# Layer normalisation of a graph kernel: statistics kept in place of rows, rows made by ScalarE, conv1's weights prepared earlier

## The reference, cut to what matters

```python
h = maximum(layernorm(x), 0)                      # per node, eps 1e-5
# layer 0, a gated unit with two inputs
c = relu(bn1(conv1d(h.T, conv1_w)))               # 1 tap: 256x256
c = relu(bn2(conv1d(c, conv2_w, pad=8)) + h.T).T  # 17 taps
s = h @ w_se.T + b_se                             # 3 values a node
A = exp(-|s_n - s_m|^2) * adj
nmp = A @ relu(h @ w_msg.T + b_msg)
gi = concat(c, nmp) @ w_ih.T + b_ih ; gh = h @ w_hh.T + b_hh
r, z = sigmoid(gi_r + gh_r), sigmoid(gi_z + gh_z)
n = tanh(gi_n + r * gh_n)
x = x + (1 - z) * n + z * h
# layer 1
g = maximum(layernorm(x), 0)
x = x + relu(g @ w[:256] + (adj @ g) @ w[256:] + bias)
```

## Time and profile before

| | |
|---|---|
| median of the runs | 1807.4 us |
| the profiled execution | 1806.16 us, span 1804.4 us |
| granted TensorE clock, mean | 0.994 |
| PE busy | 1729.2 us (96%) |
| DVE busy | 1475.5 us (82%) |
| ACT busy | 884.0 us (49%) |
| POOL busy | 594.4 us (33%) |
| DMA queue of SP | 261.94 MB, 46.1% of 16 engines' span |

### The profile page before, as it was taken

The page is one execution under the profiler, slowest core; times in us unless marked ns, Lnnn a source line. Parts: engine busy times, 40 slices in busy tenths (PEclk is TensorE's granted clock), DMA queues, the critical chain, the costliest instruction groups (busy, mean ns, idle before and its releaser), DMA issues. The chain is left out here.

```text
span 1804.4 us, 36601 instructions
## 1 busy us (share of the span) xinstructions
PE 1729.2 (96%) x12221; PEld 1139.9 (63%) x12222; DVE 1475.5 (82%) x3194; ACT 884.0 (49%) x1617; POOL 594.4 (33%) x744
## 2 busy tenths in 40 slices
PE   3779999999998999999999999999999999999997
PEld 2467777764445666666666666666666666666664
DVE  6789888862346988888888888888888888888886
ACT  4665666665344444444444444444444444444442
POOL 5688777711012222222222222222222222222221
PEclk9899999999999999999999999999999999999999
DMA  6287888769743334334334334334334334334331
GB/s 241 77 302 262 290 304 281 256 230 340 258 141 121 96 100 116 94 100 116 94 100 116 94 101 115 94 101 115 94 102 115 93 104 115 92 105 115 92 107 33
DMA packets 242827, 262.70 MB, mean 146 GB/s; under 512 B 82392, under 2 KB 178639, under 8 KB 242255
## 3 DMA queue, kind: packets, MB, share of 16 engines
q1 hardware_dynamic: 242766, 261.94, 46.1%
HBM read 154.92 MB, written 90.18 MB: 136 GB/s over the span
## 5 line engine op out<-in xcount | busy, mean ns | idle before, releaser
L1568 PE MATMUL ps_rz<-big 128*128 128x512 f16 x2304 | 560.1, 379 | 0.8 <-DVE big L1561 0.8
L1568 PEld LDWEIGHTS ps_rz<-big 128*128 128x128 f16 x2304 | 221.9, 98 | 203.0 <-DVE big L1561 1.0
L1568 PE MATMUL ps_n<-big 128*128 128x256 f16 x2304 | 314.2, 273 | 0.2
L1568 PEld LDWEIGHTS ps_n<-big 128*128 128x128 f16 x2304 | 225.1, 98 | 95.2 <-DVE big L1705 1.2
L1568 PE MATMUL ps_l<-big 128*128 128x512 f16 (+1 forms) x1536 | 272.0, 327 | 8.8 <-DVE big L1807 4.5
L1279 PE MATMUL m_ps<-big 128*128 128x512 f16 (+1 forms) x1152 | 268.3, 375 | 3.2 <-DVE big L1046 2.4
L1736 POOL TENSOR_TENSOR big<-big 128x256 f32<-128x256 f32 x128 | 97.6, 763 | 450.7 <-ACT big L1729 450.7
L1568 PEld LDWEIGHTS ps_l<-big 128*128 128x128 f16 x1536 | 149.9, 98 | 97.2 <-DVE big L1807 5.5
L1568 PE MATMUL ps_b<-big 128*128 128x256 f16 x1536 | 189.9, 273 | 2.1 <-DVE big L1636 2.1
L1711 ACT ACTIVATE big<-big,w_scale 128x512 f32<-128x512 f32 x128 | 92.6, 724 | 177.0 <-DVE big L1702 177.0
L1279 PEld LDWEIGHTS m_ps<-big 128*128 128x128 f16 x1152 | 111.9, 98 | 105.3 <-issue 2.4
(11 more groups left out here) (240 smaller groups left out, 2802.9 us busy)
## 6 DMA issues: line engine op xcount, KB each, us to landing
spectra<-ysb SPq DMA_DIRECT2D x96, 256.0 KB, 3.7
big<-spectra SPq DMA_DIRECT2D x64, 384.0 KB, 3.4
xin<-in_x SPq DMA_DIRECT2D x64, 256.0 KB, 3.4
x_normed<-front SPq DMA_DIRECT2D x64, 256.0 KB, 2.3
h_turned<-front SPq DMA_DIRECT2D x64, 256.0 KB, 3.9
big<-h_turned SPq DMA_DIRECT2D x64, 256.0 KB, 2.7
big<-in_adj SPq DMA_DIRECT2D x64, 256.0 KB, 3.4
big<-in_x SPq DMA_DIRECT2D x64, 256.0 KB, 2.8
```

Source lines behind the costliest of these rows:

```text
L1568: last = pe.matmul(dest, stationary(dl), moving(wl), start=start and n == 0, stop=stop and n == 2, **kw)
```

## The change

Four things.
1. In the filters' stage DVE makes the scales and conv1's scaled weights before `square_rows(1)`, PE turns them before it spreads the row scales, ACT copies them before its first filter tiles, and the small values per channel are made inside the loop over tiles, after its third pair.
2. POOL's part per graph is the inverse root and, in place of the rows, a bias -mean x root, two instructions of 128x1. Mean (negated and scaled) and root of every graph stay in a tile `norm`.
3. ACT makes the rows xhat in the convolution, `normalise(q+1)` at the head of its slot q. They are not stored any more; the tile `norm` is, once (1 KB a partition), at unit 6 after the slots.
4. In the gates' stage the 16 bytes a partition of `norm` are loaded a graph in place of the rows, and ACT makes the rows again (`normed_rows`), after `weighted_high`.

```diff
@@ convolution_weights, scalar
-                act.wait_ge(scales_ready, 1)
-                tile_high(0)
-                tile_high(2)
                 act.wait_ge(w1_turned, 1)
                 act.activation(w1t[:, 0, :, 0:D], pz[3][:, 0, :].rearrange("p (h o) -> p h o", o=D),
                                ACT.Copy).then_inc(w1_high, 1)
                 act.activation(bias_m[:, :], pz[3][:, 1, 0:D], ACT.Copy).then_inc(w1_high, 1)
+                act.wait_ge(scales_ready, 1)
+                tile_high(0)
+                tile_high(2)
@@ convolution_weights, vector
-                square_rows(1)
                 dve.wait_ge(sums_seen, 1)
...
+                dve.tensor_scalar(cvec[:, 0:2], V(tmp, 0), sc[:, 4:5], None, ALU.mult)
+                then(dve.tensor_scalar(cvec[:, 2:4], V(tmp, 1), sc[:, 4:5], None, ALU.mult))
+                for h in range(H):
+                    dve.tensor_scalar(w1n[:, h, :], w1n[:, h, :], cvec[:, h:h + 1], None,
+                                      ALU.mult).then_inc(w1_scaled, 1)
...
+                square_rows(1)
                 dve.wait_ge(roots_made, 2)
...
+                    if b == 2:
+                        channel_values()
@@ convolution_weights, tensor
-                pe.wait_ge(scales_placed, 2)
-                for h in range(H):
-                    last = pe.matmul(pz[2][0:ROWS_T, 1, 0:NT], spread[:, h, 0:ROWS_T], placed[:, h, :],
-                                     start=h == 0, stop=h == H - 1)
-                last.then_inc(sums_seen, 1)
                 pe.wait_ge(w1_scaled, 4)
...
+                pe.wait_ge(scales_placed, 2)
+                for h in range(H):
+                    last = pe.matmul(pz[2][0:ROWS_T, 1, 0:NT], spread[:, h, 0:ROWS_T], placed[:, h, :],
+                                     start=h == 0, stop=h == H - 1)
+                last.then_inc(sums_seen, 1)
@@ convolution, sync
-                store_xhat(0)
                 load_x(3)
                 for q in range(SLOTS):
-                    if q + 1 < graphs:
-                        store_xhat(q + 1)
...
+                    if u == 6:
+                        sp.wait_ge(norm_signed, graphs)
+                        sp.dma_start(norm_d, norm[:, :, :, :].rearrange("p g h c -> p (g h c)")).then_inc(norm_stored, 16)
@@ convolution, gpsimd
-                def normalise(f):
+                def layer_bias(f):
                     pool.wait_ge(rstd_done, f + 1)
-                    if f >= 2:
-                        pool.wait_ge(turned, f - 1)
-                        pool.wait_ge(xhat_stored[f % 2], 16 * (f // 2))
                     for t in range(H):
-                        last = pool.tensor_scalar(xhat[:, f % 2, t, :], xin[:, f % 3, t, :], meanvar[:, f % 2, t, 0:1],
-                                                  rstd[:, f % 2, t:t + 1], ALU.subtract, ALU.mult)
-                    last.then_inc(xhat_done, 1)
+                        last = pool.tensor_scalar(norm[:, f, t, 0:1], norm[:, f, t, 0:1], norm[:, f, t, 1:2], -1.0,
+                                                  ALU.mult, ALU.mult)
+                    last.then_inc(norm_signed, 1)
@@ convolution, scalar
+                def normalise(f):
+                    act.wait_ge(norm_signed, f + 1)
+                    if f >= 2:
+                        act.wait_ge(turned, f - 1)
+                    for t in range(H):
+                        last = act.activation(xhat[:, f % 2, t, :], xin[:, f % 3, t, :], ACT.Identity,
+                                              scale=norm[:, f, t, 1:2], bias=norm[:, f, t, 0:1])
+                    last.then_inc(xhat_done, 1)
...
+                normalise(0)
                 for q in range(SLOTS):
+                    if q + 1 < graphs:
+                        normalise(q + 1)
                     if q < graphs:
                         split_h(q)
@@ convolution, vector, layer_stats(f)
-                    if f >= 2:
-                        dve.wait_ge(xhat_done, f - 1)
@@ gates, sync and scalar
+            before(sp, "rows_made", t, 1, 2)
             sp.dma_start(xin[:, p, :, :], x_d[t]).then_inc(x_loaded[p], 16)
-            before(sp, "diff_done", t, H, 2)
-            sp.dma_start(xhat[:, p, :, :].rearrange("p h d -> p (h d)"), xhat_d[t]).then_inc(xhat_loaded[p], 16)
+            sp.dma_start(norm[:, p, :, :].rearrange("p h c -> p (h c)"), norm_d[t]).then_inc(norm_loaded[p], 16)
+        def normed_rows(act, t, p):
+            arrived(act, x_loaded, t, p)
+            arrived(act, norm_loaded, t, p)
+            before(act, "diff_done", t, H, 2)
+            for i in range(H):
+                last = act.activation(rows_h[:, p, i, :], xin[:, p, i, :], ACT.Identity, scale=norm[:, p, i, 1:2],
+                                      bias=norm[:, p, i, 0:1])
+            last.then_inc(S["rows_made"], 1)
...
                         weighted_high(act, t, p)
+                        normed_rows(act, t, p)
```

More of the change, by code:

```diff
@@ L414, in _ @@
-                tile_low(2)
[L415 to L431, removed]
+                tile_low(2)
+                def channel_values():
+                    then(dve.tensor_scalar(V(tmp, 9), V(tmp, 9), 2.0 ** -(W_EXP + CONV_EXP + Y_EXP) * 2 / SPAN,
+                                           sc[:, 0:1], ALU.mult, ALU.mult))
+                    dve.tensor_tensor(cvec[:, 4:6], V(tmp, 2), V(tmp, 9), ALU.mult)
+                    dve.tensor_copy(cvec[:, 6:8], V(tmp, 3))
+                    then(dve.tensor_tensor(bound[:, 0, :], V(tmp, 2), V(tmp, 8), ALU.mult))
+                    then(dve.tensor_scalar(bound[:, 0, :], bound[:, 0, :], sc[:, 0:1], 2.0 * (TAPS * D) ** 0.5,
+                                           ALU.mult, ALU.mult))
+                    dve.tensor_tensor(bound[:, 1, :], V(tmp, 3), V(tmp, 3), ALU.mult)
+                    then(dve.tensor_tensor(bound[:, 0, :], bound[:, 0, :], bound[:, 0, :], ALU.mult))
+                    then(dve.tensor_tensor(bound[:, 0, :], bound[:, 0, :], bound[:, 1, :], ALU.add))
+                    dve.tensor_tensor(cvec[:, 9:10], bound[:, 0, 0:1], bound[:, 0, 1:2], ALU.add)
@@ L477, in _, with convolution @@
                         last.then_inc(w_done, 1)
-def convolution(nc, ident, big, w1t, bias_m, dt_sb, cvec, s_all, a, xin, x_loaded, y_d, h_d, xhat_d, pair_d, w, early):
+def convolution(nc, ident, big, w1t, bias_m, dt_sb, cvec, s_all, a, xin, x_loaded, y_d, h_d, norm_d, pair_d, w, early):
     x = a["x"]
@@ L541, in convolution @@
         h_stored = [sem(f"h_stored{i}") for i in range(2)]
-        xhat_stored = [sem(f"xhat_stored{i}") for i in range(2)]
+        norm_signed = sem("norm_signed")
+        norm_stored = sem("norm_stored")
         fwd_done = sem("fwd_done")
@@ L1018, in layer_stats @@
                     for t in range(H):
-                        last = dve.bn_aggr(meanvar[:, f % 2, t, :], stats[:, f % 2, t, :])
+                        last = dve.bn_aggr(norm[:, f, t, :], stats[:, f % 2, t, :])
                     last.then_inc(stats_done, 1)
@@ L1419, in sem @@
             return ctx.enter_context(nc.semaphore(name))
-        xin, xhat, adj_in, rows = early.xin, early.xhat, early.adj_in, early.rows
+        xin, norm, rows_h, adj_in, rows = early.xin, early.norm, early.rows_h, early.adj_in, early.rows
         inv, ht, pairs = early.inv, early.ht, early.pairs
@@ L1740, in x1_rows @@
             ready(dve, "n_tanh", t, i + 1, H)
-            arrived(dve, xhat_loaded, t, p)
-            dve.scalar_tensor_tensor(out=diff[:, i, :], in0=xhat[:, p, i, :], scalar=0.0, in1=new[:, i, :],
+            ready(dve, "rows_made", t)
+            dve.scalar_tensor_tensor(out=diff[:, i, :], in0=rows_h[:, p, i, :], scalar=0.0, in1=new[:, i, :],
                                      op0=ALU.max, op1=ALU.subtract).then_inc(S["diff_done"], 1)
```

63 lines of the change are left out of this document (31 added, 32 removed).

## The result

| | before | after |
|---|---|---|
| median of the runs | 1807.66 us (4 runs) | 1889.91 us (1888.7 to 1890.4, 4 runs) |
| ratio | 1 | 1.0454, 95% interval 1.0441 to 1.0467 |
| profiled execution | 1806.16 us, span 1804.4 | 1890.4 us, span 1888.2 |
| PE busy, granted clock | 1729.2 us, 0.994 | 1754.9 us, 0.986 |
| DMA of SP's queue | 261.94 MB | 228.64 MB |

A forecast was written before the change was run, and what follows sets the result against it. PE, busy 96%, bounded the old kernel; a new loop of waits would outlast its slots. 1806.2 + 81.6 (slots) + 0.9 (beginning) - 1.0 (filters) = 1887.7, about 1888 as median; 8-of-10 range 1850 to 1915.

The forecast's parts named there:

- The ring's path and length: Convolution slots: waits from DVE's aggregate through GpSimd's bias, ACT's normalise and split_h, back to DVE, 5.91 us every slot.
- The held add: GpSimd's add L832: held by DVE's two-SBUF-input instruction, 0.544 against 0.194; the bias pair stays short, taken as 0.55 us.
- The rival of the short loop: Convolution slots: add not held, bias pair and normalise shorter, so 5.05 us a slot, +28, time 1835; chance 0.12.
- The number of turns: Convolution: the new loop of waits comes round 62 times from split_h(1) to split_h(63).
- The extra of heavy slots: Heavy convolution slots: split_y ahead of add_bias adds about 0.6 in one of four, mean 0.17 us a slot.
- The sum of the slots: Convolution, split_h(1) to split_h(63): 374.1 us where the old kernel takes 292.5, so +81.6.
- The beginning: Up to split_h(1): the first turn comes earlier, but split_h(1) now waits for normalise(2); +0.9 us.
- The stores: Convolution and unit 6: storing no rows, and one small store at unit 6 instead, is worth 0.
- The gates' rows: Gates' stage: ACT's 0.91 us a graph fits in 1.48 idle, 0; rival without cover +58, time 1945, chance 0.03.
- The filters' stage: Filters' stage: PE starts 2.3 to 3.7 earlier, channel_values cost 1.6 to 3.0 in DVE's loop; net -1 us.
- the 1887.7 of the sum: Whole kernel: profiled 1806.2 + 81.6 + 0.9 - 1.0 us; about 1888 as median of runs.
- The rival of the clock: Light convolution slots: TensorE drops to 1.2 GHz, 7.1 us a slot, +20, time 1908 or more; chance 0.10.

The follow-up runs named there:

- e2_pool: The kernel after the change, but GpSimd makes the convolution's rows as before: 1808.29 us, 1.0002 of the kernel before.
- e8_rows_twice: The kernel after the change, with ACT making each graph's rows twice in the gates' stage: 1892.21 us, 1.0468 of the kernel before.
- e7_pool_values: As e1_behind, but GpSimd makes the values per channel after its last pair of tiles, not DVE inside its loop: 1801.96 us, 0.9965 of the kernel before.
- e1_behind: The kernel after the change, with split_h(q) ahead of normalise(q+1) on ACT: 1805.53 us, 0.9987 of the kernel before.
- e4_stats_first: The kernel after the change, with layer_stats(q+2) ahead of split_h(q) on DVE, ACT's order kept: 1823.79 us, 1.0083 of the kernel before.
- e6_early_alone: The kernel before with only the change's filters' stage: 1810.10 us, 1.0009, against 1808.68 for the kernel before beside it.

## Why the prediction was right, step by step
- **The ring's path and length.** 5.91 forecast, 5.94 measured. The bias took 0.53 (0.55 taken); normalise from SBUF 1.00 (0.91 taken, from the form that reads PSUM; it came out near the upper end of the 0.60 to 1.02 considered: 593 ns each and 560 from PSUM); the hand-offs were those of the earlier trace rows within 0.03. Two small misses of opposite sign.
- **The held add.** L833 has 0.54 as before, since it still starts beside DVE's L1047, and 0.20 in the three turns at the start where it does not. The bias pair takes 0.50, but not for the reason given: in light slots no DVE instruction runs beside it, since L1054, which was L1046, ends at 127.35 and the pair starts at 127.34. The reason is tested only in heavy slots, half of which have an instruction with one input in PSUM beside the whole pair, and there it holds:
```profile
303.80 0.68 DVE L1059 SCALAR_TENSOR_TENSOR ysb<-m_ps,ysb 128x512 f16<-128x512 f32 x1
303.88 0.50 POOL L841 TENSOR_SCALAR norm<-norm 128x1 f32<-128x1 f32 x2
```
  The rival of the short loop, which needed L832 at 0.19, falls.
- **The number of turns.** The sum has 62 turns; the ring has 61. Behind the normalise of graph 63 no other comes, so nothing stands ahead of split_h(63), and the last distance is 3.82 us and not 5.9:
```profile
450.66 1.09 ACT L918 ACTIVATE front<-xin,norm 128x256 f32<-128x256 f32 x2 [0.53 <-POOL norm L841]
451.66 0.57 ACT L927 ACTIVATE front<-turn_ps 128x512 f16<-128x512 f32 x1
...
455.48 0.59 ACT L927 ACTIVATE front<-turn_ps 128x512 f16<-128x512 f32 x1
```
- **The extra of heavy slots.** 0.17 on average forecast; 5.94, 5.94, 5.95 and then 6.54 measured, 0.60 in one slot of four, the one with split_y ahead of add_bias. The mean of the 44 turns is 6.12, so 0.18.
- **The sum of the slots.** 374.1 forecast, 455.48 - 81.33 = 374.15 measured. That this agrees to a tenth is luck: 0.03 too little on each of 61 turns is 2, and the turn too many gave 2 back.
- **The beginning.** +0.9 forecast. From the first statistic to split_h(1) it is 10.27 us and was 9.42: +0.85.
- **The stores.** 0 forecast. They were not run by themselves; together with the rest of the change they are worth 0 (e2_pool).
- **The gates' rows.** 0 forecast for the sum, 0.0 measured in 1209.4 us. That they would cost 58 us without that idle time is doubtful: the 0.38 us a graph that weren't covered in e8_rows_twice cost a small part of their length.
- **The filters' stage.** The step that failed in sign: -1 forecast, +0.4 measured in the profile (71.06 against 70.67 for the first statistic), and +0.7 on average over the eight traces that have this stage (-0.2 to +1.7). PE's first product came at 26.70, 4.5 us early where I had 2.3 to 3.7: L409's successor took 0.62 with GpSimd idle, not 1.94. But I charged channel_values only their own time, at most 3.0; on DVE, which sets the pace of that loop, they cost 3.7, 2.1 of their own and 1.6 of slower low parts behind them (e7_pool_values). The loop also takes 1.2 more without them: 0.6 from the first product to the second group (8.02 for 7.43), and 0.6 behind it (24.42 in e7_pool_values, 23.82 before); why is open. -4.5 + 3.7 + 1.2 is the +0.4.
- **The tail**, +1.3, was in no step. The last products wait for DVE and a DMA as before, but in the last 20 us the granted clock is 0.72 where it was 0.88; the product at 1870.04 takes 2.47 where its fellow took 1.48, and the one behind it 4.64 for 4.25. The change's gates' stage doesn't bring it: the first of the two takes 1.48 in e1_behind and e4_stats_first and 2.74 in e2_pool, which all have that stage, and 2.35 in e6_early_alone, which hasn't. So it differs from trace to trace; what decides it is open.
- **What the sum missed.** The filters' stage (1.4) and the tail (1.3) are the 2.7 us by which the profiled execution, 1890.4, lies above the 1887.7 of the sum; -0.4 between split_h(63) and the gates' stage, which was in no step either, is made up by the 0.4 by which the two executions differ more in their times (84.2) than in their spans (83.8).
- **The rival of the clock.** It was half there: 0.91 in the light stretch (0.96 before). It cost nothing there, since no term of the ring is PE's and PE waited 28.8 us in 17 waits for DVE in these slots.

## What to carry to other kernels
When a job is given to another engine, don't add up that engine's load; write down what now stands behind the new wait in its queue, and follow it until it comes back to what the wait is for. If it comes back within one turn of the loop, the period is at least the sum of the hand-offs, however idle the engines are; if it comes back after two turns, half that sum. One call moved behind its neighbour can be worth more than the whole change. A short chore on the engine that sets the pace of a loop costs at least its own time, and here 1.6 us more behind it, so it belongs on an engine that is idle then, even where the instructions are a little slower (2.4 us on GpSimd for 2.1 on DVE here).

## What the runs showed of the hardware that I had not expected
- ACT's Identity over 128x256 f32 with pointer scale and bias takes 593 ns from SBUF and 560 from PSUM: SBUF is not the faster source for it.
- GpSimd needs 2.78 us for a multiplication of 128x1024 f16 by a constant, 2.7 times ACT's 1.04, and yet 1.22 for 128x256 f32 with two pointer scalars.
- The same wait of PE, 2.85 us at the same place of the filters' stage, was followed by different clocks: from 40.0 to 46.4 the granted clock was 0.73 after the change, 0.53 in e1_behind and 1.00 in e2_pool. Behind a wait of 0.85 us, a group earlier, it was 1.00 after the change (34.72 to 38.30).
